# Expert phase of a fused attention and mixture-of-experts kernel: shared pairs in another order, and other steps for the late choice

## What is computed

```
shared = silu(x @ sg_w.T) * (x @ su_w.T) @ sd_w.T
probs  = sigmoid(x @ router_w.T + routing_bias)      # 8 experts
topk_p, topk_idx = top_k(probs, 2); topk_p /= sum(topk_p)
routed = sum over the two chosen experts e of
         topk_p * ((silu(x @ wg[e].T) * (x @ wu[e].T)) @ wd[e].T)
out    = layernorm(x + shared + routed)
```

## Time and profile before

| what | value |
|---|---|
| median of three runs | 795.93 us |
| profiled execution, its own time | 798.8 us |
| its span | 797.1 us |
| TensorE (matmul) busy | 618.7 us, 78% |
| DVE / ScalarE / POOL busy | 513.3 / 432.4 / 374.0 us |
| expert phase | about 591 us to the end |
| shared pairs ahead of / behind the routed ones | 4 / 6 |

### The profile page before, as it was taken

The page is one execution under the profiler, slowest core; times in us unless marked ns, Lnnn a source line. Parts: engine busy times, 40 slices in busy tenths (PEclk is TensorE's granted clock), DMA queues, the critical chain, the costliest instruction groups (busy, mean ns, idle before and its releaser), DMA issues. The chain is left out here.

```text
span 797.1 us, 12128 instructions
## 1 busy us (share of the span) xinstructions
PE 618.7 (78%) x3926; PEld 339.9 (43%) x3926; DVE 513.3 (64%) x1331; ACT 432.4 (54%) x589; POOL 374.0 (47%) x419
## 2 busy tenths in 40 slices
PE   2378988897988796898786778787687983899990
PEld 1222332243533242544243334356565751666690
DVE  2567664577975587896669784568655750533794
ACT  4456877765676765566753564633623520344454
POOL 5456433535432534423414676413573356555651
PEclk9978998999999997999988788989999995899995
DMA  9136645000000000000000010000022122224532
GB/s 272 45 109 217 219 164 192 13 1 1 1 2 1 1 14 0 14 11 5 14 1 15 17 45 25 25 1 0 4 77 56 51 75 71 58 67 104 194 106 79
DMA packets 38125, 47.23 MB, mean 59 GB/s; under 512 B 8960, under 2 KB 35232, under 8 KB 37408
## 3 DMA queue, kind: packets, MB, share of 16 engines
q1 hardware_dynamic: 26976, 35.11, 14.6%
q0 software_dynamic: 4352, 9.05, 3.4%
q10 hardware_dynamic: 6736, 2.30, 1.1%
HBM read 35.30 MB, written 28.98 MB: 81 GB/s over the span
## 5 line engine op out<-in xcount | busy, mean ns | idle before, releaser
L892 ACT ACTIVATE prob<-ps_s 128x1024 f32<-128x1024 f32 x320 | 309.8, 1024 | 164.7 <-PE ps_s L1244 110.5
L1281 PE MATMUL ps_v<-prob,va 128*32 128x512 f32 x1152 | 170.3, 676 | 5.4 <-POOL prob L782 4.7
L1244 PE MATMUL ps_s<-qs,ks 32*128 32x512 f16 x576 | 91.1, 404 | 47.2 <-ACT prob L892 44.2
L1514 POOL DMA_INDIRECT y_rows<-y,to_row x72 | 70.3, 976 | 61.4 <-DVE y L1635 46.1
L782 POOL TENSOR_SCALAR_AFFINE_SELECT prob<-prob 128x1024 f32<-128x1024 f32 x64 | 70.1, 1115 | 52.9 <-ACT prob L892 52.7
L1047 DVE STREAM_TRANSPOSE sums<-ps_v 128x512 f32<-128x512 f32 x62 | 44.3, 714 | 77.1 <-PE ps_v L1281 41.5
L1244 PEld LDWEIGHTS ps_s<-qs,ks 32*128 32x128 f16 x576 | 22.0, 91 | 140.2 <-ACT prob L892 107.5
L1742 PE MATMUL ps_gu<-weights,rows_t 128*128 x144 | 72.0, 625 | 12.2 <-issue 10.4
L1547 ACT ACTIVATE gated<-ps_gu 128x512 f32<-128x512 f32 x46 | 27.4, 597 | 93.8 <-PE ps_gu L1742 40.6
L1275 PE MATMUL ps_v<-prob,vd 128*128 128x256 f32 (+1 forms) x292 | 65.8, 377 | 13.6 <-DVE marked L1067 13.2
L1275 PEld LDWEIGHTS ps_v<-prob,vd 128*128 128x128 f32 x292 | 54.2, 210 | 31.6 <-DVE prob L1074 16.6
(11 more groups left out here) (229 smaller groups left out, 1051.4 us busy)
## 6 DMA issues: line engine op xcount, KB each, us to landing
x_rows<-in_blank SPq DMA_DIRECT2D x8, 2112.0 KB, 9.4
rows<-x_rows SPq DMA_DIRECT2D x72, 66.0 KB
chosen_y<-y_rows SPq DMA_DIRECT2D x8, 512.0 KB, 4.3
weights<-in_weights SPq DMA_DIRECT2D x1, 3456.0 KB, 13.7
out<-result ACTq DMA_DIRECT2D x8, 256.0 KB, 2.3
marked<-in_hidden SPq DMA_DIRECT2D x3, 512.0 KB, 5.8
r_in<-in_hidden SPq DMA_DIRECT2D x6, 256.0 KB, 3.0
y_rows<-y,to_row POOLq DMA_INDIRECT x72
```

Source lines behind the costliest of these rows:

```text
L892: act.activation(probs_at(n, 0, SLOT_COLS), scores_at(n, 0, SLOT_COLS), ACT.Exp, scale=HD ** -0.5 / GAIN ** 2).then_inc(exped, 1)
L1244: last = pe.matmul(scores_at(n, j * BANK, BANK).rearrange("p (r q) -> p r q", r=REP), ks[b % QUERY_BATCHES][rows, kt * P:(kt + 1) * P], qs ...
L1281: last = pe.matmul(bank[g * VW:(g + 1) * VW, :, :], va[b % VALUE_BATCHES][:, kt, g, :], probs_at(n + g // 2, g % 2 * BANK, BANK).rearrange ...
L1514: pool.indirect_dma_start(y_rows, bass.IndirectOffsetOnAxis(ap=to_row[:, m, t:t + 1], axis=0), y[m][:, t, :], None).then_inc(y_sent[group_ ...
```

## The change

One shared pair (8) and not four comes first. Pair 9 comes between routed pairs 19 and 20, that is between the second and third part. The other eight come last, in the order 10, 11, 4, 5, 12, 13, 14, 15. So routed pair m is at step m + 1 up to pair 19 and at step m + 2 from pair 20 on; before it was at step m + 4. The steps of the late choice are one less each; the dispatch of the last part comes behind the sends of nine pairs instead of six. As pair 0 is now at step 1, its register load on TensorE is written ahead of the loop. `IN_TIME` was chunk 2 alone; it is now chunks 2, 5, 6 and 7. By the new tables the steps at which chunks 0 to 7 get their results are 38, 40, 46, 41, 44, 45, 47, 48; before they were 41, 43, 49, 45, 47, 47, 49, 50.

```diff
-SHARED_FIRST = [8, 9, 10, 11]
-SHARED_LAST = [12, 13, 14, 15, 4, 5]
-SEQUENCE = ([("shared", j) for j in SHARED_FIRST] + [("routed", m) for m in range(PAIRS)] + [("shared", j) for j in SHARED_LAST])
+SHARED_FIRST, SHARED_BETWEEN, SHARED_LAST = [8], [9], [10, 11, 4, 5, 12, 13, 14, 15]
+SEQUENCE = ([("shared", j) for j in SHARED_FIRST] + [("routed", m) for m in range(SHARE_PAIRS[FINAL - 1])]
+            + [("shared", j) for j in SHARED_BETWEEN] + [("routed", m) for m in range(SHARE_PAIRS[FINAL - 1], PAIRS)]
+            + [("shared", j) for j in SHARED_LAST])
...
-LATE_BEGIN, LATE_AT = 1, 4
+LATE_BEGIN, LATE_AT = 0, 3
 PICK_AT = {1: {"blocks": 4, "ends": 4, "starts": 5, "past": 5, "rows": 6, "experts": 6},
-           2: {"prob": 8, "first": 8, "second": 9, "third": 9, "weights": 9, "totals": 11, "scan": 11, "slots": 11, "slot1": 12,
-               "slot2": 12, "blocks": 13, "ends": 14, "starts": 15, "past": 16, "rows": 17, "experts": 18}}
-TURN_AT = {c: SHARED_AT[c * CT // 2] - 3 if c * CT // 2 in SHARED_LAST else SHARED_FIRST.index(c * CT // 2) // 2 - 1
+           2: {"prob": 7, "first": 7, "second": 8, "third": 8, "weights": 8, "totals": 10, "scan": 10, "slots": 10, "slot1": 11,
+               "slot2": 11, "blocks": 12, "ends": 13, "starts": 14, "past": 15, "rows": 16, "experts": 17}}
+TURN_AT = {c: SHARED_AT[c * CT // 2] - 3 if c * CT // 2 in SHARED_LAST else -1
...
-GATHERED_AT = {0: 34, 1: 36, 3: 38, 4: 40, 2: 41, 5: 42, 6: 46, 7: 47}
+GATHERED_AT = {0: 31, 1: 33, 3: 34, 2: 36, 4: 37, 5: 39, 6: 43, 7: 45}
 LAST = 2
-IN_TIME = [f for f, when in GATHERED_AT.items() if f not in FILLED and when <= SHARED_AT[2 * f] + LAST]
+IN_TIME = [f for f, when in GATHERED_AT.items() if f not in FILLED and when < SHARED_AT[2 * f] + LAST]
...
-END_STEPS = {f: 6 if f in FILLED else 2 for f in END_AT} | {4: 6, 5: 4}
-POWER_BEFORE = {END_AT[f] - SHARED_AT[SHARED_FIRST[-1]] - LAST: f for f in FILLED}
-FINAL_SENDS = 6
+END_STEPS = {f: 6 for f in FILLED} | {4: 6, 5: 4, 2: 3, 6: 2, 7: 1}
+POWER_BEFORE = {END_AT[f] - len(SHARED_FIRST + SHARED_BETWEEN) - LAST: f for f in FILLED}
+FINAL_SENDS = 9
...
+            load_weights(0)
             for c in turned_at(-1):
                 turn_tokens(c)
```

## The result

| | before | after |
|---|---|---|
| median, run in turns on one chip (16 runs each) | 796.5 us | 800.24 us |
| lowest to highest | 794.23 to 800.61 | 795.94 to 805.92 |
| profiled execution, its span | 798.8, 797.1 us | 797.73, 795.9 us |
| first gate of the expert phase to the end of the span | 204.1 us | 206.6 us |
| last product of the attention part to the end of the span | 206.6 us | 210.7 us |

A forecast was written before the change was run, and what follows sets the result against it. TensorE was taken as the bound from step to step, except a 26.0 us hold-up. Gate of step 38 at 752.6 plus tail 36.8 gave 789.4 against 797.1, 7.7 less; 795.9 - 7.7 = 788.2 us, range 770 to 796.

The forecast's parts named there:

- The head: Start of the expert phase: late tokens' chain slides 3.2 us sooner, their gate comes at 612.2; gain 0.7 us.
- The hold-up: TensorE stopped during POOL's unbroken series of sends from about 643: again 22 sends and 26 us, no change.
- The price for SP: SP's row loads for pairs 16 to 19, slow inside POOL's series: no time charged for them.
- rival 2: The hold-up goes, as SP's loads leave POOL's series: 24 us more saved, 764; chance 0.12, plus 0.10 for a shorter one.
- The second stretch: From the late tokens' gate to the first shared gate behind the routed pairs (step 38): that gate at 752.6.
- The tail: From the gate of step 38 to the end: 36.8 us, 1.7 shorter than before with two more shared pairs.
- rival 3: Tail hidden no better, DVE waiting at step 43 for chunk 6's chosen y, or head starves: both 794 to 797; chance 0.08.
- Rival 1: POOL's series grows, holding TensorE longer: 2.5 us per further pair, 801 with five; chance 0.13.

The follow-up runs named there:

- powers put apart: Changed kernel with POOL's powers of chunks 0, 1, 3 moved ahead of pairs 29, 31, 33: 0.9996 of the kernel before with hold-up; 1.0000 and 0.9997 without.
- spare power: Changed kernel with chunks 6 and 7's roots on DVE, plus one unused POOL power waiting for chunk 7's variance: 771.72 us, 1.0033 of the kernel before, without hold-up.
- last root: Changed kernel with only chunk 7's inverse root moved from POOL to DVE, in seven instructions: 1.0004 of the kernel before, with hold-up.
- long breaks: Changed kernel with a spare-tile power on POOL ahead of every four of the 16 dispatches: 1.0067 of the kernel before, with and without hold-up.

## Why the prediction was wrong

*The head* held to 2 us. The register load was forecast to shift the first gate by 0.9 us. TensorE's idle time there grew by 1.2 (1.90 for 0.73), in every profile of a changed kernel, and from the last product of attention to the first gate it is 4.1 us, forecast 3.4. The gate behind the late tokens came 23.05 us behind that product (608.26 - 585.21), forecast 21.7. It took 3.63 us and not 1.9, at a mean granted clock of 0.55 of full (608.2 to 612 us), that is mostly at the lower level; TensorE had been busy for 2.4 of the 4.2 us before.

*The hold-up* held in all its parts: a row of 22 (2 + 16 + 4) from 641.3 us, TensorE held 25 us (646.3 to 671.5), forecast 26. The price for SP was rightly nothing: its eight loads were issued in 4.92 us from 640.6, ahead of the stop, and the hold-up was the same. What I weighed of the Trainium skill ("DMA: Bandwidth & Descriptors", section "SWDGE vs HWDGE vs iDMA") says less than I made of it: transfers issued from SP or ScalarE don't use the rings that GpSimd writes, and so don't suffer when VectorE locks GpSimd out of them. That a slow SP has nothing to do with POOL's sends was my own step. The traces speak against the step, not against the page: eight loads in 21.79 us inside the row and in 4.92 ahead of the stop, with SP's register instructions as late as its loads. That the new order would shed the hold-up (rival 2) fell.

*The second stretch.* The first shared gate behind pair 35 came 165.7 us behind the last product of attention (750.95 - 585.21), forecast 162.1 (752.6 - 590.5): 3.6 us late in all. Of that 0.7 arose ahead of the first gate, 0.6 up to the gate above, and 1.7 is that gate itself.

*The tail* is the step that failed: 44.9 us from the gate of step 38 to the end (750.95 to 795.9) instead of 36.8.

- 5.5 us: gates of steps 38 to 42 took 16.4 us, not 3.06 + 3 x 2.62 = 10.9. I had noted in the earlier trace rows that TensorE isn't held where sends stand in fours with a power between, and then read the new `POWER_BEFORE` for its count alone. Its entries follow `END_AT`, which the change moved; they left eight sends in a row. Shown by the powers put apart, which give 5.1 us back; the last 0.4 is not the hold-up, as these steps take 11.3 us without it too.
- 4.1 us: the end was put at the landing of the last store. POOL's DRAIN, 9.63 us from the start of its last power, was the real end: 795.7 against 791.5, or 4.1 us when the 0.3 us between SP's DRAIN and the end of a span that SP ends is taken off. It bounded the kernel before too, so no tail could become shorter than that power's start + 9.8 us. I had seen the last row of ScalarE and 3.85 us behind it, and took these for the store. Shown by the spare power and by the last root.
- The work itself was 1.5 us quicker than forecast: from the gate of step 42 to SP's DRAIN 24.2 us, with 0.3 to close 24.4 (forecast 25.9). Some 1.0 of it is the last term of my sum: the 3.85 us behind the last row, read from the earlier trace rows, held the DRAIN of the kernel before; landing and close alone are 2.8 (788.94 to 791.5, and 0.3). DVE was never late for chosen y (rival 3 fell), and only one set of results stood behind the last shift.

The sum: -7.7 + 3.6 + 5.5 + 4.1 - 1.5 = +4.0 us; the profile shows +4.1 and the medians +3.7. Rival 1 named the right mechanism, a longer row, in the wrong place: the first row didn't grow, a second one arose. That its 801 us, for five pairs more in the first row, lies so near the measured 800.24 is chance. Without hold-up the changed kernel is 1.9 us quicker (0.9978, interval up to 1.0001), and no more, as the DRAIN ends it there too (from 755.1, 9.63 us, while SP drains at 760.6). Whether that is all that holds it back I can't settle: the kernel before has no profile of that condition.

## What to carry to other kernels

Look at the closing instructions of the block, not only at the last row of work: an engine's DRAIN can be the end, and then a shorter tail gives nothing until that engine's last computation is earlier. When a table of steps moves, write down anew what each queue issues in a row, small instructions included; one of 1 us that seemed a cost was what kept a queue from harm. Measure a phase from an instruction that the change can't have moved: from the first gate the profile hid 1.6 us of what the change cost. And time a change under both conditions of the machine, if it has two: the ratio was 1.005 in one and 0.998 in the other.

## What the runs showed of the hardware

- Under one condition that isn't the kernel's and lasted a whole session, a row of POOL's indirect DMAs 1.26 us apart stops TensorE, DVE and ScalarE from 4 to 8 us into the row until 1 to 3.5 us behind it: 25 us for 22 sends, 5 us for 8. Rows of four held TensorE 1.5 us at most (one of them, in one profile of the kernel before; the others nothing), and four and two with 0.71 us of idle between them (powers apart) nothing. Under the other condition, some 40 in a row did nothing. It is worth 28 us of 796 in the kernel before.
- Under the first condition SP's register instructions, 29 ns long, took up to 0.70 us and more (up to 1.40 with the long breaks), and in the long row of the kernel before 20 of 23 instructions of SP started 0.7 us or a multiple of it behind the one before; under the other the longest took 42 ns. Read this first to know which condition a profile has.
- A row ended with 1.26 us from the end of a send to the start of the next (a power of 1.0 us between) or with 1.70 us of idle alone, and not with 0.39 us (a product of 0.2 us between).
- What the condition is, and why it acts so, stays open; chips 7 and 11 showed both.
- POOL's DRAIN at the end of the block took 9.61 to 9.63 us from the start of its last power in every profile; ScalarE's took 0.16, DVE's 0.2, SP's 0.007. The span ended 0.1 to 0.3 us behind the last of them.
- A register load put ahead of TensorE's first instruction of a phase cost 1.2 us there: idle time of 1.88 to 1.90 us in all eighteen profiles with it, 0.73 in both without.
